# Softplus in a Mamba and mixture-of-experts kernel: two ScalarE operations in place of three

## The chip, the cores and the metric

The kernel runs on one core of a Trainium2 chip. The metric is the device time of one execution in microseconds (us). A core has TensorE (PE in the profile), VectorE (DVE), ScalarE (ACT), GpSimd (POOL) and SyncE (SP), which issues the DMAs; each works through its own list of instructions in the order in which the program gives them, and they wait for each other through semaphores.

## The reference

The input is x of 8 sequences (batches) of 1024 tokens and 256 channels, in float32. A layer has two parts: a two-way Mamba block and a mixture of experts, each between layernorms and with a residual. The change touches the Mamba block alone, and in it one line, the softplus:

```python
x = silu(causal_depthwise_conv(xz_half, conv_w, conv_b))
dbc = x @ Wx.T
delta, Bm, Cm = dbc[..., :64], dbc[..., 64:80], dbc[..., 80:]
delta = jax.nn.softplus(delta @ Wdt.T + b_dt)
dA = exp(delta[..., None] * A)                       # A = -exp(A_log)
bx = delta[..., None] * Bm[:, :, None, :] * x[..., None]
h = dA_t * h + bx_t                                  # for each token, 16 states
y = einsum("ben,bn->be", h, c) + Dp * x
```

## The kernel before

The 8 batches with two directions each make 16 passes w; w is 0 to 15. In a pass, 512 channels lie as 4 tiles c of 128 partitions, and the 1024 tokens as 2 halves s of 512 columns. For each pass and each of the 16 states n the engines run a loop over the 4 channel tiles. ScalarE makes `decay` (L1692), which is exp of delta times A, half by half. GpSimd makes `drive` (L1977, L1983), which is delta times x (the tile `xu`) times a row of B. VectorE runs the scan over the tokens from both (`h`, L1454, L1463 and L1466). TensorE transposes the states (`h_t`, L1238), and VectorE (L1475) or, for every third token block about, ScalarE and GpSimd together (`scaled` L1713, `y` L1995) add the transposed states, weighted with C, to `y`. There are 3 buffers of `decay`, 3 of `drive` and 3 of `h_t`, so each of these engines can run only a little ahead of the next.

Between these instructions stands all other work: the projections, the convolution, the experts, the norms, and the softplus. Its place is fixed by a table of numbers written out by hand (`AT`), one number for each piece and engine; a piece stands in an engine's list at that slot. One softplus is a piece for a pass, a channel tile and a half, so there are 16 x 4 x 2 = 128 of them. It has four steps on three engines. TensorE's `dt_mm` (L1294) writes a PSUM bank (`side`, of which there are 2 for all this work). ScalarE's `softplus` (L1791, L1793, L1795) reads it and leaves a part of the result in `log_parts`, which the profile shows as `prep_work`. VectorE's `delta` (L1513) reads both, writes delta and so frees the bank. GpSimd's `u_mul` (L2007) multiplies x by delta for the two halves of a tile in one instruction; from pass 1 on delta also goes to memory and back, to be loaded for `decay`. In pass 0 all this stands ahead of the first scans, at the start of the program; later passes are prepared while the scans of the pass before run.

ScalarE can hold several tables of functions, one at a time. The kernel loads the one with Exp and Ln after each use of another.

Of the kernel before, what the change touches and what calls it, by code (L numbers as in the profile page):

```python
# [9 lines left out]
ALU = mybir.AluOpType  # L10
ACT = mybir.ActivationFunctionType
# [540 lines left out]
        873, 1018, 1020, 1022, 1025, 1175, 1176, 1177, 1180, 1240, 1241, 1242, 1243],  # L552
    "tok_apply": [1154, 1155, 1167, 1169],
}

TAIL_USE = 1153

# [22 lines left out]
class Plan:  # L580
# [23 lines left out]
    def nth(self, piece, *index):  # L604
        return self.at[piece, index]
# [152 lines left out]
def mamba_moe(nc, x, w_in_t, chan, wx_t, wdt_t, w_out_t, router_w, router_b, w1, b1_t, w2, b2, out):  # L758
# [47 lines left out]
    nth = plan.nth  # L806


    bank_of, bank_before, filled = {}, {}, {}
# [26 lines left out]
    with ctx:  # L836
# [78 lines left out]
        log_parts = xz_pad[:, PAD:PAD + L]  # L915
# [19 lines left out]
        side = [ctx.enter_context(nc.psum_tensor(f"side{i}", [P, BANK], F32)) for i in range(N_SIDE)]  # L935
# [36 lines left out]
        soft_step = sem("soft_step")  # L972
# [450 lines left out]
        def dve_program(dve):  # L1423
# [77 lines left out]
            def side_piece(piece, index):  # L1501
                if piece == "delta":
                    w, c, s = index
                    half_of = slice(s * BANK, (s + 1) * BANK)
# [4 lines left out]
                    elif w % 2 and w > 1:  # L1509
                        dve.wait_ge(done["u_mul"], nth("u_mul", w - 1, EC - 1))  # L1510
                        dve.wait_ge(done["delta_store"], 16 * nth("delta_store", w - 1, EC - 1))
                    into = prep_half if w else delta[:, c, :]
                    op = dve.e.scalar_tensor_tensor(out=into[:, half_of], in0=side[bank_of["dt_mm", index]][:, :],  # L1513
                                                    scalar=0.0, in1=log_parts[:, half_of], op0=ALU.max, op1=ALU.add)
                elif piece in ("tok_stats", "ln_stats"):
                    kind, at, j = index
                    src, dst, first, n, (stats, mv, rstd, shift) = norm_io(kind, at)
# [8 lines left out]
                    for tb in (first + 2 * j, first + 2 * j + 1):  # L1526
                        op = dve.e.bn_stats(stats[:, tb, :], src[:, tb, :])
                elif piece in ("tok_var", "ln_var"):
# [4 lines left out]
                    for tb in range(first, first + n):  # L1533
                        op = dve.e.bn_aggr(mv[:, tb, :], stats[:, tb, :])
                elif piece == "tap":
                    w, c, s = index
# [3 lines left out]
                    for k in range(1, TAPS):  # L1540
                        at = PAD - (TAPS - 1 - k) + s * BANK
                        into = bank[:, :] if k + 1 < TAPS else xu[:, 0, c, s * BANK:(s + 1) * BANK]
                        op = dve.e.scalar_tensor_tensor(out=into, in0=xz_of(w, c)[:, at:at + BANK],
                                                        scalar=chan_col(0, c, CHAN_CONV_W + k), in1=bank[:, :],
                                                        op0=ALU.mult, op1=ALU.add)
# [3 lines left out]
                elif piece == "gate":  # L1549
                    b, s, c = index  # L1550
# [3 lines left out]
                    op = dve.e.tensor_tensor(its, side[bank_of["y_turn", index]][:, :], its, ALU.mult)  # L1554
                elif piece == "res_add":
                    b, s, j = index
# [6 lines left out]
                    else:  # L1563
                        dve.wait_ge(own_res_in[s], 16 * QB // 2)
                    op = dve.e.tensor_tensor(acc_of(b)[:, at:at + 2, :].rearrange("p b d -> p (b d)"), bank[:, :],
                                             tokens_of(b, at, 2), ALU.add)
                elif piece == "peak":
# [8 lines left out]
                    op = dve.e.tensor_tensor(logits[:, :, :], logits[:, :, :], wide(), ALU.subtract)  # L1576
                elif piece == "top1":
                    b, = index
                    dve.wait_ge(done["probs"], nth("probs", b))
                    if b:  # L1580
# [6 lines left out]
                    op = dve.e.scalar_tensor_tensor(out=mix[:, :, 0:E], in0=sel1[:, :, :], scalar=-2.0,  # L1587
                                                    in1=logits[:, :, :], op0=ALU.mult, op1=ALU.add)
                elif piece == "top2":
# [6 lines left out]
                    op = dve.e.tensor_tensor(mix[:, :, 0:E], logits[:, :, :], both[:, :, :], ALU.mult)  # L1596
                elif piece == "slots":
# [5 lines left out]
                    if b:  # L1603
                        for i in range(N_FOUND):
# [14 lines left out]
                                                       in1=ranks, op0=ALU.mult, op1=ALU.add))  # L1619
# [3 lines left out]
                    op = dve.e.tensor_copy(slot_i[:, :, :], slot_f[:, :, :])  # L1623
                elif piece == "owners":
# [11 lines left out]
                    for r, sel in enumerate((sel1, sel2)):  # L1636
                        ordered(dve.e.tensor_tensor(cand[:, :, :], logits[:, :, :], sel[:, :, :], ALU.mult))
                        op = dve.e.tensor_reduce(share[:, b % 2, r, :], cand[:, :, :], AX_X, ALU.add)
                        if r + 1 < TOP:
                            ordered(op)  # L1640
                elif piece == "comb":
# [5 lines left out]
                    op = dve.e.tensor_tensor(its, side[bank_of["comb_mm", index]][:, :], its, ALU.add)  # L1647
                elif piece == "fin_add":
                    b, s, j = index
# [4 lines left out]
                    op = dve.e.tensor_tensor(acc_of(b)[:, at:at + 2, :].rearrange("p b d -> p (b d)"), bank[:, :],  # L1654
                                             x1_of(b)[:, at:at + 2, :].rearrange("p b d -> p (b d)"), ALU.add)
# [16 lines left out]
        def act_program(act):  # L1672
# [42 lines left out]
            def side_piece(piece, index):  # L1715
                if piece == "xn_copy":
                    b, s, c = index
# [3 lines left out]
                    op = act.e.copy(xn_t[:, c, s * BANK:(s + 1) * BANK], side[bank_of["xn_turn", index]][:, :])  # L1721
                elif piece == "xz_copy":
                    b, c, s = index
# [6 lines left out]
                    op = act.e.copy(xz_of(2 * b, c)[:, PAD + s * BANK:PAD + (s + 1) * BANK], side[bank_of["proj", index]][:, :])  # L1730
                elif piece == "conv_copy":
                    w, c, s = index
                    d = w % 2
                    act.wait_ge(done["conv_mm"], nth("conv_mm", w, c, s, 1))
                    if w >= 2:
                        act.wait_ge(drive_made, (w - 1) * UNITS)
                    op = act.e.activation(xu[:, d, c, s * BANK:(s + 1) * BANK], side[bank_of["conv_mm", (w, c, s)]][:, :],
                                          ACT.Identity, bias=chan_col(d, c, CHAN_CONV_B))
                elif piece == "tap0":
                    w, c, s = index  # L1740
# [5 lines left out]
                    op = act.e.activation(bank[:, :], xz_of(w, c)[:, at:at + BANK], ACT.Identity,  # L1746
                                          scale=chan_col(0, c, CHAN_CONV_W), bias=chan_col(0, c, CHAN_CONV_B))
                elif piece == "neg_a":
# [5 lines left out]
                    op = act.e.mul(neg_a[:, :, :, :], neg_a[:, :, :, :], -1.0)  # L1754
                elif piece == "silu_x":
                    w, s = index
# [5 lines left out]
                    op = act.e.activation(its, its, ACT.Silu)  # L1762
                    if w or s == NH - 1:
                        act.e.preload_act_table_set("natural_log_exp_and_others")
                elif piece == "dbc_copy":
                    w, s = index
# [5 lines left out]
                    op = act.e.copy(dbc[0:NP, s * BANK:(s + 1) * BANK], side[bank_of["dbc_mm", index]][0:NP, :])  # L1772
                elif piece == "c_copy":
                    w, s = index
                    act.wait_ge(done["c_turn"], nth("c_turn", w, s))
                    if w >= 2:
                        act.wait_ge(summed, summed_to((w - 1) * TILES - 1))
                        act.wait_ge(tile_scaled, pooled_to((w - 1) * TILES - 1))
                    op = act.e.copy(c_col[:, w % 2, s * QB:(s + 1) * QB, :],
                                    side[bank_of["c_turn", index]][:, 0:QB * NP].rearrange(  # L1780
                                        "p (q k) -> p q k", q=QB)[:, :, DTR + N:NP])
                elif piece == "softplus":
                    w, c, s = index
                    log_part = log_parts[:, s * BANK:(s + 1) * BANK]
# [2 lines left out]
                        act.wait_ge(done["delta"], nth("delta", w, c - 1, s))  # L1787
                    elif w % 2 == 0:
                        act.wait_ge(done["xz_store"], 16 * nth("xz_store", w // 2, EC - 1))
                    done_before = 2 * (nth("softplus", w, c, s) - 1)  # L1790
                    act.e.activation(log_part, side[bank_of["dt_mm", index]][:, :], ACT.Abs).then_inc(soft_step, 1)  # L1791
                    act.wait_ge(soft_step, done_before + 1)
                    act.e.activation(log_part, log_part, ACT.Exp, scale=-1.0).then_inc(soft_step, 1)  # L1793
                    act.wait_ge(soft_step, done_before + 2)
                    op = act.e.activation(log_part, log_part, ACT.Ln, bias=1.0)  # L1795
                elif piece == "z_copy":
                    b, s, c = index
# [7 lines left out]
                    op = act.e.copy(z_of(b, s)[:, c, :], side[bank_of["z_mm", index]][:, :])  # L1805
                elif piece == "z_silu":
                    b, s = index
                    act.wait_ge(done["z_copy"], nth("z_copy", b, s, EC - 1))
                    op = act.e.activation(z_of(b, s), z_of(b, s), ACT.Silu)
                    act.e.preload_act_table_set("natural_log_exp_and_others")  # L1810
                elif piece == "out_copy":
# [9 lines left out]
                    op = act.e.mul(acc_of(b)[:, tile_of(b, i), :], side[bank_of["out_mm", index]][:, 0:D], 0.5)  # L1821
                elif piece == "xn2_copy":
                    b, s, c = index
# [7 lines left out]
                    op = act.e.copy(xn2_of(b)[:, c, t:t + BANK], side[bank_of["xn2_turn", index]][:, :])  # L1831
                elif piece in ("tok_apply", "ln_apply"):
# [6 lines left out]
                    if kind in ("post", "fin"):  # L1839
                        into = free_bank(act, piece, index)[:, :].rearrange("p (r d) -> p r d", d=D)  # L1840
                    elif kind == "pre":
                        into = tokens_of(at[0], first + 2 * j, 2).rearrange("p (r d) -> p r d", d=D)
                    else:
                        into = dst[:, 2 * j:2 * j + 2, :]
                    for r in range(2):
                        tb = first + 2 * j + r
                        op = act.e.activation(into[:, r, :], src[:, tb, :], ACT.Identity, scale=rstd[:, tb:tb + 1],
                                              bias=shift[:, tb:tb + 1])
                elif piece == "probs":
                    b, = index  # L1850
                    act.wait_ge(done["peak"], nth("peak", b))
                    op = act.e.activation(logits[:, :, :], logits[:, :, :], ACT.Exp)
                elif piece == "mix_copy":
# [6 lines left out]
                    op = act.e.copy(mix_t[:, q * BANK:(q + 1) * BANK], side[bank_of["mix_turn", index]][0:NX, :])  # L1860
                elif piece == "h1_bias":
# [5 lines left out]
                    else:  # L1867
                        act.wait_ge(done["y_turn"], nth("y_turn", b, 0 if b == LAST else NH - 1, EC - 1, 1))
                    op = act.e.activation(h1_of(b)[:, m, :], side[bank_of["h1_mm", index]][:, :], ACT.Identity,
                                          bias=b1_sb[:, m, NX - 1:NX])  # L1870
                elif piece == "gelu":
                    b, g = index
                    act.wait_ge(done["h1_bias"], nth("h1_bias", b, g, HC - 1))
                    op = act.e.activation(h1_of(b)[:, :, :], h1_of(b)[:, :, :], ACT.Gelu)
                    if (b, g) != (LAST, NH - 1):
                        act.e.preload_act_table_set("natural_log_exp_and_others")
                elif piece == "eo_copy":
# [4 lines left out]
                    op = act.e.copy(acc_of(b)[:, tb:tb + 2, :].rearrange("p b d -> p (b d)"),  # L1882
                                    side[bank_of["eo_mm", index]][:, :])
                elif piece == "share_diag":
# [7 lines left out]
                    for r in range(TOP):  # L1892
                        op = act.e.mul(diag[:, i % 2, r, :], ident[:, :], share[:, b % 2, r, tile_of(b, i):tile_of(b, i) + 1])
                elif piece == "bias_copy":
                    b, = index
                    act.wait_ge(done["bias_mm"], nth("bias_mm", b))
                    if b:
                        act.wait_ge(done["r1_copy"], nth("r1_copy", b - 1, BLOCKS - 1))
                    op = act.e.copy(b1_blocks[:, :, :].rearrange("p m j -> p (m j)"),
                                    side[bank_of["bias_mm", index]][:, 0:HC * SLOTS])  # L1900
                elif piece == "xs_copy":
                    b, G, c = index
# [28 lines left out]
                elif piece == "rgelu":  # L1931
# [4 lines left out]
                    op = act.e.activation(its, its, ACT.Gelu)  # L1936
# [501 lines left out]
```

## Time and profile before

| | |
|---|---|
| median of 3 runs | 4375.84 us (4371.07 to 4379.16) |
| the profiled execution's own time | 4368.3 us |
| its span in the profile | 4367.0 us |
| busy: PE, DVE, POOL, ACT | 82%, 85%, 83%, 72% |

The profile is of one execution. Its own time stands 1.3 us over its span and 7.5 us under the median. Busy shares are those of the whole span. The chain of work that ended last is followed back from the last instruction, at each step to what released it or to the instruction before it on its engine. In a timeline, the brackets give the idle time of the engine ahead of an instruction and what ended it.

### The profile page before, as it was taken

The page shows a single profiled execution, that of the slowest core. Times are in us where ns is not written, and L with a number is a line of the kernel's source. Part 1 is how long each engine was busy: PE and PEld are TensorE (multiplying, and loading weights), DVE is VectorE, ACT ScalarE, POOL GpSimd, SP SyncE. Part 2 cuts the span into 40 slices and gives each one's busy share as a digit, 9 for nine tenths or more (in the row PEclk, how much of TensorE's full clock was granted, in tenths as well). Part 3 has the DMA queues.
Part 4 walks back from the last instruction along what each step waited for, and adds up shares of the span by engine and source line. Part 5 has one row for each costly group of instructions (what it writes and reads, how often), then busy time and mean ns, then how long its engine had stood idle before and what let it go on. Part 6 is the DMA issues. An engine that isn't in the chain of part 4 may idle for free.

```text
span 4367.0 us, 58183 instructions
## 1 busy us (share of the span) xinstructions
PE 3587.1 (82%) x18192; PEld 2572.1 (59%) x18192; DVE 3692.7 (85%) x4568; ACT 3162.5 (72%) x5296; POOL 3645.2 (83%) x2205
## 2 busy tenths in 40 slices
PE   5677687988879897798879887798987989878887
PEld 2444455666546655576555774556755666557766
DVE  5899998998988979889898988988989897989720
ACT  5667576887768867688766887768876787768643
POOL 5899988998888988889888989888997898889721
PEclk8778797999979999899979998899998999889988
DMA  5232232566335654357433674445643566426555
GB/s 176 85 111 97 100 134 81 197 197 216 128 116 172 205 198 130 110 182 240 159 130 131 195 235 144 142 140 188 229 157 109 169 201 221 137 95 215 181 178 186
DMA packets 374654, 700.87 MB, mean 160 GB/s; under 512 B 31809, under 2 KB 205386, under 8 KB 370378
## 3 DMA queue, kind: packets, MB, share of 16 engines
q1 hardware_dynamic: 362058, 663.59, 46.1%
q0 software_dynamic: 12288, 33.57, 2.3%
q8 instruction: 145, 2.38, 0.2%
q14 instruction: 163, 1.34, 0.1%
HBM read 527.72 MB, written 169.35 MB: 160 GB/s over the span
## 4 chain that ended last, share of the span: by engine, by line
PE 27%; DVE 23%; POOL 20%; issue 14%; ACT 13%; DMA 3%; DVEq 0%; SPq 0%; POOLq 0%; ACTq 0%
POOL drive L1977 10%; DVE h L1466 8%; DVE h L1463 7%; PE h_t L1238 5%; PE side L1272 4%; DVE y L1475 4%; ACT decay L1692 3%; POOL y L1995 3%; PE side L1411 3%; POOL xs_dram L2053 2%; PE side L1403 2%; PE side L1327 1%; PE side L1300 1%; PE side L1279 1%; ACT scaled L1713 1%
## 5 line engine op out<-in xcount | busy, mean ns | idle before, releaser
L1977 POOL TENSOR_TENSOR drive<-xu,b_row 128x1024 f32<-128x1024 f32 x960 | 2263.0, 2362 | 284.9 <-DVE h L1466 185.1
L1692 ACT ACTIVATE decay<-delta,neg_a 128x512 f32<-128x512 f32 x2048 | 1397.1, 692 | 674.4 <-DVE h L1466 400.5
L1238 PE MATMUL h_t<-ident,h 128*128 128x128 f32 x8192 | 1281.9, 300 | 513.8 <-DVE y L1475 209.0
L1238 PEld LDWEIGHTS h_t<-ident,h 128*128 128x128 f32 x8192 | 1049.0, 155 | 897.9 <-DVE y L1475 303.0
L1475 DVE SCALAR_TENSOR_TENSOR y<-h_t,c_col,y 128x512 f32<-128x512 f32 x1368 | 996.0, 728 | 131.8 <-PE h_t L1238 127.6
L1995 POOL TENSOR_TENSOR y<-y,scaled 128x512 f32<-128x512 f32 x616 | 784.8, 1274 | 71.1 <-ACT scaled L1713 69.6
L1466 DVE TENSOR_TENSOR_SCAN h<-decay,h,drive 128x512 f32<-128x512 f32 x512 | 652.4, 1274 | 32.8 <-ACT decay L1692 20.9
L1466 DVE TENSOR_TENSOR_SCAN h<-decay,drive 128x512 f32<-128x512 f32 x512 | 618.2, 1207 | 51.0 <-POOL drive L1977 26.6
L1463 DVE TENSOR_TENSOR_SCAN h<-decay,h,drive 128x512 f32<-128x512 f32 x448 | 571.6, 1276 | 57.5 <-ACT decay L1692 47.2
L1463 DVE TENSOR_TENSOR_SCAN h<-decay,drive 128x512 f32<-128x512 f32 x448 | 541.3, 1208 | 67.0 <-POOL drive L1977 35.2
L1713 ACT ACTIVATE scaled<-h_t,c_col 128x512 f32<-128x512 f32 x616 | 415.6, 675 | 101.6 <-PE h_t L1238 101.5
L1272 PE MATMUL side<-prep_work,conv_diag 128*128 128x512 f32 x960 | 458.5, 611 | 10.8 <-DMA prep_work<-xz_dram 4.5
L1411 PE MATMUL side<-expert_w,work 128*128 128x256 f32 x1304 | 336.2, 409 | 30.1 <-ACT xn_t L1911 10.5
L1403 PE MATMUL side<-xn_t,expert_w 128*128 128x128 f32 x2608 | 335.7, 278 | 25.1 <-ACT work L1929 7.1
L1403 PEld LDWEIGHTS side<-xn_t,expert_w 128*128 128x128 f32 x2608 | 312.6, 193 | 40.6 <-ACT work L1929 12.0
L1411 PEld LDWEIGHTS side<-expert_w,work 128*128 128x128 f32 x1304 | 258.7, 207 | 77.3 <-ACT xn_t L1911 12.1
L1272 PEld LDWEIGHTS side<-prep_work,conv_diag 128*128 128x128 f32 x960 | 174.1, 196 | 167.4 <-issue 157.9
L2065 POOL DMA_INDIRECT work<-ys_dram,slot_i x128 | 123.0, 961 | 164.2 <-DMA ys_dram<-work 109.3
L1929 ACT ACTIVATE work<-side,b_blocks 128x128 f32<-128x128 f32 x644 | 183.3, 373 | 32.2 <-PE side L1403 31.3
L1294 PE MATMUL side<-dbc,wdt_sb 97*128 97x512 f32 x256 | 158.3, 715 | 24.0 <-ACT xn_t L1911 10.9
L1983 POOL TENSOR_TENSOR drive<-xu,b_row 128x1024 f32<-128x1024 f32 x64 | 151.0, 2365 | 12.2 <-DVE h L1454 11.3
L2053 POOL DMA_INDIRECT xs_dram<-work,slot_i x112 | 110.3, 984 | 58.4 <-issue 30.5
(297 smaller groups left out, 4366.7 us busy)
## 6 DMA issues: line engine op xcount, KB each, us to landing
expert_w<-in_w SPq DMA_DIRECT2D x350, 512.0 KB, 4.5
b_row<-b_dram SPq DMA_DIRECT2D x240, 512.0 KB, 4.1
x_dram<-xu SPq DMA_DIRECT2D x16, 2048.0 KB, 7.7
delta_dram<-prep_work SPq DMA_DIRECT2D x60, 512.0 KB, 4.2
delta<-delta_dram SPq DMA_DIRECT2D x60, 512.0 KB, 4.6
ys_dram<-work SPq DMA_DIRECT2D x40, 512.0 KB, 6.4
work<-xs_dram SPq DMA_DIRECT2D x38, 512.0 KB, 4.6
h<-in_w SPq DMA_DIRECT2D x34, 512.0 KB, 4.8
```

What stands on the lines that cost most here:

```text
L1238: t = pe.e.transpose(h_t[i % N_H_T][:, c * P:(c + 1) * P], its_h[:, c, :], ident[:, :])
L1272: mm = pe.e.matmul(bank[:, :], conv_diag[:, k, :], xz_pad[:, at:at + BANK], start=(k == 0), stop=(k == TAPS - 1))
L1403: mm = pe.e.matmul(bank[:, m * P:(m + 1) * P], wi[:, k, m * P:(m + 1) * P], xn2_t[:, k, at:at + P], start=(k == 0), stop=(k == DC - 1))
L1411: mm = pe.e.matmul(bank[:, q % 2 * D:(q % 2 + 1) * D], h1_blocks(b, G)[:, q, m, :], wo[:, m, :], start=(m == 0), stop=(m == HC - 1))
L1463: return dve.e.tensor_tensor_scan(o[:, ::-1], its_decay[:, ::-1], v[:, ::-1], before, ALU.mult, ALU.add)
L1466: return dve.e.tensor_tensor_scan(o, its_decay, v, before, ALU.mult, ALU.add)
L1475: dve.e.scalar_tensor_tensor(out=y[:, tb, :], in0=h_t[i % N_H_T][:, :], scalar=c_n, in1=y[:, tb, :], op0=ALU.mult, op1=ALU.add).then_inc(s ...
L1692: act.e.activation(decay[:, i % N_DECAY, :], delta[:, c, its], ACT.Exp, scale=neg_a[:, c, w % 2, n:n + 1]).then_inc(decay_made, 1)
L1713: act.e.mul(into, h_t[i % N_H_T][:, :], c_col[:, w % 2, tb, n:n + 1]).then_inc(tile_scaled, 1)
L1977: op = pool.e.tensor_tensor(drive[:, k % N_DRIVE, :], xu[:, w % 2, c, :], b_row[:, row % N_B_ROW, :], ALU.mult)
L1995: pool.e.tensor_tensor(y[:, tb, :], y[:, tb, :], scaled[:, at % N_SCALED, :], ALU.add).then_inc(gathered, 1)
L2053: pool.e.indirect_dma_start(out=xs_dram, out_offset=bass.IndirectOffsetOnAxis(ap=slot_i[:, r, tb:tb + 1], axis=0), in_=tokens_of(b, tb, 1) ...
```

## The change

Before, softplus(x) was max(x, 0) + ln(1 + exp(-|x|)): ScalarE made |x| out of PSUM, then Exp with the scale -1, then Ln with the bias 1, and VectorE put max(x, 0) to it. Now it is max(min(ln(1 + exp(x)), 17), x): ScalarE makes Exp out of PSUM and then Ln, and VectorE takes the smaller of that and 17, and then the larger of that and x. Over 17, where the result is x to within what float32 shows, x is the larger. In VectorE's instruction the PSUM bank was the first tensor operand and is now the second.

```diff
--- before.py
+++ after.py
@@ -553,6 +553,8 @@
     "tok_apply": [1154, 1155, 1167, 1169],
 }
 
+SOFT_MAX = 17.0
+
 TAIL_USE = 1153
 
 EMPTIED_BY = {"xn_turn": "xn_copy", "proj": "xz_copy", "dbc_mm": "dbc_copy", "c_turn": "c_copy", "dt_mm": "delta",
@@ -1510,8 +1512,8 @@
                         dve.wait_ge(done["u_mul"], nth("u_mul", w - 1, EC - 1))
                         dve.wait_ge(done["delta_store"], 16 * nth("delta_store", w - 1, EC - 1))
                     into = prep_half if w else delta[:, c, :]
-                    op = dve.e.scalar_tensor_tensor(out=into[:, half_of], in0=side[bank_of["dt_mm", index]][:, :],
-                                                    scalar=0.0, in1=log_parts[:, half_of], op0=ALU.max, op1=ALU.add)
+                    op = dve.e.scalar_tensor_tensor(out=into[:, half_of], in0=log_parts[:, half_of], scalar=SOFT_MAX,
+                                                    in1=side[bank_of["dt_mm", index]][:, :], op0=ALU.min, op1=ALU.max)
                 elif piece in ("tok_stats", "ln_stats"):
                     kind, at, j = index
                     src, dst, first, n, (stats, mv, rstd, shift) = norm_io(kind, at)
@@ -1787,11 +1789,8 @@
                         act.wait_ge(done["delta"], nth("delta", w, c - 1, s))
                     elif w % 2 == 0:
                         act.wait_ge(done["xz_store"], 16 * nth("xz_store", w // 2, EC - 1))
-                    done_before = 2 * (nth("softplus", w, c, s) - 1)
-                    act.e.activation(log_part, side[bank_of["dt_mm", index]][:, :], ACT.Abs).then_inc(soft_step, 1)
-                    act.wait_ge(soft_step, done_before + 1)
-                    act.e.activation(log_part, log_part, ACT.Exp, scale=-1.0).then_inc(soft_step, 1)
-                    act.wait_ge(soft_step, done_before + 2)
+                    act.e.activation(log_part, side[bank_of["dt_mm", index]][:, :], ACT.Exp).then_inc(soft_step, 1)
+                    act.wait_ge(soft_step, nth("softplus", w, c, s))
                     op = act.e.activation(log_part, log_part, ACT.Ln, bias=1.0)
                 elif piece == "z_copy":
                     b, s, c = index
```

ScalarE's rows below are the first two pieces `softplus` (pass 0, tile 0, both halves) and the first `decay` behind them, each with the semaphores that it waits for. Before:

```order
L1791 ACTIVATE prep_work<-side 128x512 [waits s_xz_store,s_dt_mm]
L1793 ACTIVATE prep_work<-prep_work 128x512 [waits soft_step]
L1795 ACTIVATE prep_work<-prep_work 128x512 [waits soft_step]
L1791 ACTIVATE prep_work<-side 128x512 [waits s_dt_mm]
L1793 ACTIVATE prep_work<-prep_work 128x512 [waits soft_step]
L1795 ACTIVATE prep_work<-prep_work 128x512 [waits soft_step]
L1692 ACTIVATE decay<-delta,neg_a 128x512 [waits s_delta,s_neg_a]
```

Now:

```order
L1792 ACTIVATE prep_work<-side 128x512 [waits s_xz_store,s_dt_mm]
L1794 ACTIVATE prep_work<-prep_work 128x512 [waits soft_step]
L1792 ACTIVATE prep_work<-side 128x512 [waits s_dt_mm]
L1794 ACTIVATE prep_work<-prep_work 128x512 [waits soft_step]
L1694 ACTIVATE decay<-delta,neg_a 128x512 [waits s_delta,s_neg_a]
```

One row of each piece has gone, and nothing else stands elsewhere: ScalarE's list is 128 instructions shorter, it has the same table loads, and TensorE, VectorE, GpSimd and SyncE have the same instructions in the same order, but for the operands of VectorE's `delta`. (Line numbers behind the first hunk are 2 higher, and those behind the second 1 lower.)

## Rows read from the trace of the kernel before

**Rows 1.** The page's head and its section 1: busy time of each engine, share, instructions
```profile
span 4367.0 us, 58183 instructions
...
PE 3587.1 (82%) x18192; PEld 2572.1 (59%) x18192; DVE 3692.7 (85%) x4568; ACT 3162.5 (72%) x5296; POOL 3645.2 (83%) x2205
```

**Rows 2.** The chain of work that ended last: share of the span by engine
```profile
PE 27%; DVE 23%; POOL 20%; issue 14%; ACT 13%; DMA 3%; DVEq 0%; SPq 0%; POOLq 0%; ACTq 0%
```

**Rows 3.** Waits: who waited for whom, total us, times, longest us
```profile
ACT decay L1692 <- DVE h L1466: 400.5, 432, 5.0
...
ACT decay L1692 <- DVE h L1463: 234.4, 298, 7.3
```

**Rows 4.** ACT's groups by form: count, busy us, mean ns, idle before
```profile
L1692 ACT ACTIVATE decay<-delta,neg_a 128x512 f32<-128x512 f32 x2048 | 1397.1, 692 | 674.4 <-DVE h L1466 400.5 <-DVE h L1463 234.4 <-DVE h L1454 27.5
...
L1793 ACT ACTIVATE prep_work<-prep_work 128x512 f32<-128x512 f32 x128 | 80.7, 631 | 4.1
L1795 ACT ACTIVATE prep_work<-prep_work 128x512 f32<-128x512 f32 x128 | 80.7, 631 | 4.0
L1791 ACT ACTIVATE prep_work<-side 128x512 f32<-128x512 f32 x128 | 75.5, 590 | 23.2 <-PE side L1294 22.8
```

**Rows 5.** Timeline of ACT at its second softplus: start us, us, what
```profile
54.70 0.63 ACT L1795 ACTIVATE prep_work<-prep_work 128x512 f32<-128x512 f32 x1
55.23 0.58 ACT L1791 ACTIVATE prep_work<-side 128x512 f32<-128x512 f32 x1
55.84 0.63 ACT L1793 ACTIVATE prep_work<-prep_work 128x512 f32<-128x512 f32 x1
56.51 0.63 ACT L1795 ACTIVATE prep_work<-prep_work 128x512 f32<-128x512 f32 x1
```

**Rows 6.** DVE's groups by form: count, busy us, mean ns, idle before
```profile
L1475 DVE SCALAR_TENSOR_TENSOR y<-h_t,c_col,y 128x512 f32<-128x512 f32 x1368 | 996.0, 728 | 131.8 <-PE h_t L1238 127.6 <-POOL y L1995 2.5
...
L1513 DVE SCALAR_TENSOR_TENSOR prep_work<-side,prep_work 128x512 f32<-128x512 f32 x120 | 81.3, 680 | 12.1 <-ACT prep_work L1795 11.9
...
L1543 DVE SCALAR_TENSOR_TENSOR xu<-h,chan_sb,side 128x512 f32<-128x512 f32 x8 | 6.0, 748 | 0.3
```

**Rows 7.** Timeline of POOL, start of the program: start us, us, what, idle before
```profile
57.94 2.35 POOL L2007 TENSOR_TENSOR xu<-xu,delta 128x1024 f32<-128x1024 f32 x1 [37.58 <-DVE delta L1513]
60.25 1.04 POOL L2034 TENSOR_TENSOR conv_diag<-ident,chan_sb 128x512 f32<-128x512 f32 x1
62.77 2.35 POOL L2007 TENSOR_TENSOR xu<-xu,delta 128x1024 f32<-128x1024 f32 x1 [1.49 <-DVE delta L1513]
...
70.70 4.66 POOL L2007 TENSOR_TENSOR xu<-xu,delta 128x1024 f32<-128x1024 f32 x2
75.31 9.25 POOL L1977 TENSOR_TENSOR drive<-xu,b_row 128x1024 f32<-128x1024 f32 x4
```

**Rows 8.** Timeline of DVE, the same stretch
```profile
72.00 0.67 DVE L1513 SCALAR_TENSOR_TENSOR delta<-side,prep_work 128x512 f32<-128x512 f32 x1
...
77.76 1.22 DVE L1466 TENSOR_TENSOR_SCAN h<-decay,drive 128x512 f32<-128x512 f32 x1 [3.91 <-POOL drive L1977]
```

**Rows 9.** The chain that ended last: its first and last piece of L1793
```profile
54.04 0.64 ACT prep_work L1793
...
3736.77 0.64 ACT prep_work L1793
```

**Rows 10.** Timeline, instructions that end ACT's part of the chain, with idle before them
```profile
1451.88 1.28 DVE L1463 TENSOR_TENSOR_SCAN h<-decay,h,drive 128x512 f32<-128x512 f32 x1 [2.34 <-ACT decay L1692]
...
2512.42 0.69 DVE L1513 SCALAR_TENSOR_TENSOR prep_work<-side,prep_work 128x512 f32<-128x512 f32 x1 [2.39 <-ACT prep_work L1795]
...
3550.66 1.28 POOL L1995 TENSOR_TENSOR y<-y,scaled 128x512 f32<-128x512 f32 x1 [2.59 <-ACT scaled L1713]
```

**Rows 11.** Timeline of DVE: two places where it has next to no idle time
```profile
2159.06 0.69 DVE L1513 SCALAR_TENSOR_TENSOR prep_work<-side,prep_work 128x512 f32<-128x512 f32 x1
...
3202.65 1.21 DVE L1466 TENSOR_TENSOR_SCAN h<-decay,drive 128x512 f32<-128x512 f32 x1
```

## The prediction

> **What bounds the kernel now.** The page's head comes first: no engine is the bound of the whole span. VectorE is busy for 85% of it, GpSimd for 83%, TensorE for 82% and ScalarE for 72% [rows 1]. The chain of work that ended last says how this is to be read: it passes from engine to engine, and 13% of the span in it is ScalarE's [rows 2]. Next come the waits. ScalarE, ahead of a `decay`, waits 400.5 + 234.4 us for a scan, 432 + 298 times [rows 3]. That is 730 of its 2048 `decay` instructions [rows 4]: at about one in three (0.36) ScalarE is early, and what it does faster there only lengthens its wait. At the others it works through a queue, and something may wait for it. So the 128 shorter softplus pieces are not worth their busy time. They are worth what lies on the chain, and of that only as much as the engine that waits for ScalarE had idle.
>
> **What the change removes.** One softplus piece is three instructions on ScalarE: L1791 out of PSUM, mean 590 ns, then L1793 and L1795 out of SBUF, 631 ns each [rows 4]. Each waits for the one before. In the timeline L1793 starts at 55.84 us and L1795 at 56.51, so a dependent step takes 0.67 us from start to start; L1791, which depends on nothing just before it, starts at 55.23, 0.10 before L1795 of the piece before ends (54.70 + 0.63) [rows 5]. What stays is one instruction out of PSUM and one out of SBUF. If Exp out of PSUM takes what L1791 takes, the loss of a step is 0.66 us a piece (631 ns and some 30 ns until the next starts), 128 x 0.66 = 84.5 us of ScalarE's time in all. The trace has no Exp out of PSUM. Its bounds are L1791's 590 ns below, and above the 692 ns of `decay`, an Exp out of SBUF with a scale for each partition [rows 4]; by the upper one a piece saves 0.66 - 0.10 = 0.56 us. I take 590: shape, source and immediate scale are those of L1791.
>
> The Trainium skill, ScalarE: Activation LUTs, "Same chain, other wiring", has every function at one element per cycle and lane. By this rule Exp out of PSUM costs what the absolute value costs, and a piece saves 0.66 us. The trace agrees as far as it goes: L1793 (Exp) and L1795 (Ln) both show 631 ns [rows 4]. The same page, "What ACT_TABLE_LOAD costs", gives 186 ns + 0.833 ns per element for an ACTIVATE with immediate scale and bias, an estimate of 612 ns at 512 columns, whatever the source. By that a piece would save 0.64 us; the measured 590 and 631 decide.
>
> **What the change adds.** No instruction and no table load: the order has as many loads as before. VectorE's `delta` has min and max for max and add, and its PSUM operand is the second instead of the first. Before it takes 680 ns. The nearest rows with a PSUM tensor first and second are L1475 with 728 ns and L1543 with 748, both with a scalar for each partition [rows 6]. Their difference is 20 ns; a price under nothing I exclude, since 680 ns is already the least of the three. I take 20 ns, with 0 as the other bound. All 128 of them make 2.6 us. I count a quarter as on the path, since VectorE holds 23% of the chain [rows 2]: 0.7 us against the change.
>
> **The start of the program.** Here ScalarE sets the pace, since the first scans wait for softplus. GpSimd's first `u_mul` starts at 57.94 us, behind two pieces. It then makes a `conv_diag`, sits idle for 1.49 us and starts the second `u_mul` at 62.77, behind four pieces [rows 7]. With four steps fewer that one's delta comes 4 x 0.66 = 2.64 us earlier. GpSimd's own queue allows 2 x 0.66 + 1.49 = 2.81 us, which is more, so the delta decides: 2.6 us. After that GpSimd has no idle time until 75.31 + 9.25 = 84.56 [rows 7], and VectorE waits for its `drive` (3.91 us before 77.76) [rows 8], so the gain is kept. One thing could take from it. The fourth `u_mul` starts at 70.70 + 2.33 = 73.03 and would start at 70.4. Its delta, the eighth, stands on VectorE between scans at 72.00 [rows 8]. It moves with the scans to 69.4 and ends at 70.0, 0.4 us in time.
>
> **The passes behind it.** In the chain L1793 is met 23 times of 128, first at 54.04 and last at 3736.77 us [rows 9]. Two of the 23 are in the start. For each of the other 21 I went forward along the chain to the first instruction of another engine, and read that engine's idle time before it. This is what its own queue lets it gain. At 15 it is enough for all the pieces ahead: 2.34, 2.39 and 2.59 us in the rows shown [rows 10], where one or two pieces save 0.66 or 1.32. That is 15 x 0.66 = 9.9 us. At the other 6 there is little: five have about 0.1 us or none, as at 2159.06, where VectorE has just ended an instruction, and at 3202.65 [rows 11], and one 0.39; together 0.6 us. So the queues of the next engines leave 10.5 of 21 x 0.66 = 13.9 us. Two things take from that. ScalarE, when earlier, meets a wait for a scan buffer between softplus and the end of its stretch: at most the share of 0.36 from above. And a path that ran beside the chain, and that I cannot follow, may end later than the shortened one. I take a quarter off for both, a choice between none and 0.36: 7.9 us.
>
> **The sum.** 2.6 + 7.9 - 0.7 = 9.8 us. The profiled execution's own time is 4368.3 us, so its counterpart would be 4358.5. It stands 7.5 us under the median of the runs shown, and the same gain on that median gives 4375.84 - 9.8 = 4366.0 us, 0.22% less. About 0.2%, 8.7 us, is what a measurement of this kernel can tell from no change, so the forecast lies almost on the edge.
>
> **Rivals.**
> *The slack swallows it.* ScalarE, 72% busy and early at a third of its `decay`s, is not what most stages wait for; VectorE and GpSimd, at 85% and 83%, go on as before. Then the start remains with 2.6 us, and the 20 ns of `delta` cost between 0.7 and 2.6: a gain of 0 to 2, with a little from the passes up to 6 us; 4370 to 4376. For it speaks that only 23 of 128 are on the chain, and that six of those meet a full queue. Against it: 15 places with over 0.66 us idle behind them.
> *All of it counts.* All 23 steps come out of the time, 15.2 us, and the start gives 1.3 more than its two steps in the chain (2.64 against 1.32): 16.5 us, 4359.3. For it: the places are those at which ScalarE was late. Against: the six full queues.
> *Slower.* VectorE's `delta` with the PSUM bank as second operand takes much longer than 680 ns. It frees the bank for TensorE, and GpSimd waits for it. With a quarter of 128 on the path, 32 of them, against a gain of 10.5 us otherwise, the change is without effect at 10.5 / 32 = 0.33 us more for each, and slower by 0.2% at 0.60 us more. If it went in two passes, and took 1.36 us, the time would be 4375.84 - 10.5 + 32 x 0.68 = 4387. The rows with PSUM second (748 ns) speak against it [rows 6].
> *The step is not saved.* Exp out of PSUM would have to take 590 + 660 ns for that; nothing in the rows, with 692 ns at most for such an instruction, speaks for it, and it has no chance of its own.
>
> **How the numbers follow.** A gain near the sum, 6 to 14 us: 0.54. Swallowed: 0.27. All of it: 0.13. Slower: 0.06. The likeliest gives 4366.0. Of its 0.54, rather more than two thirds, 0.37, lie beyond 8.7 us. With 0.13 that is 0.50 for faster; 0.44 is left for no difference, and 0.06 for slower. The range goes from a gain of 17.5, which is all of it and 1 us for the spread of medians, to the upper end of the swallowed case: 4358 to 4376. What it leaves out is the slower case and the edges of the others.
>
> **What the profile afterwards would show.** ScalarE with 5168 instructions and 80 us less busy time; the Exp out of PSUM near 590 ns, at most 692; `delta` between 680 and 700 ns; the second `u_mul` on GpSimd at about 60.1 us, and everything to 84 us earlier by 2.6. ScalarE's waits for scans should grow by most of the 84 us, since only a tenth of it is gained. VectorE's wait for L1795's successor, 11.9 us in pass 1 on [rows 6], should shrink by half or more. The prediction is wrong if the start gives less than 2 us, which would mean that another wait stands right behind; or if the rest of the gain is under 3 us or over 14, which would mean that the idle time of the next engine is no measure of what is gained.

## The result

The changed kernel takes 4364.86 us in the median of 20 runs (4357.38 to 4373.52), the kernel before 4375.07 us in 20 runs (4371.07 to 4383.15). The ratio is 0.9974 with a 95% interval of 0.9967 to 0.9981: 11.4 us less, 8.3 to 14.4. A second comparison, 12 runs against 19, gave 0.998 (0.9969 to 0.999), 8.7 us less, 4.4 to 13.6. All gains here are (1 - ratio) times the median of before; the ratio is formed from all the runs and not from the two medians, so the difference of the medians is up to 4 us off it (10.2 us in the first comparison). Two executions that took over twice the usual time, one of the kernel before (9046.76 us) and one of a kernel below (11018.61 us), are left out of all medians. The forecast was 9.8 us, 4366.0 on the median shown.

The profiled execution's span is 4363.0 us. These are the page's head, its section 1 and the chain's shares by engine, for the changed kernel; they answer to [rows 1, 2].

```profile
span 4363.0 us, 58055 instructions
...
PE 3581.1 (82%) x18192; PEld 2572.4 (59%) x18192; DVE 3692.2 (85%) x4568; ACT 3088.2 (71%) x5168; POOL 3644.6 (84%) x2205
...
PE 27%; DVE 22%; POOL 21%; issue 14%; ACT 12%; DMA 3%; DVEq 0%; SPq 0%; another core or an unknown queue 0%; POOLq 0%; ACTq 0%
```

ScalarE has 128 instructions and 74.3 us of busy time less. The other engines have as many instructions as before. Of 74 us, 11 reach the time.

The groups of ScalarE and `delta` on VectorE from pass 1 on, by form, answer to [rows 4, 6]. The last row is from the view of one line: least, median and longest duration in ns, then the first and the last start in us.

```profile
L1694 ACT ACTIVATE decay<-delta,neg_a 128x512 f32<-128x512 f32 x2048 | 1399.0, 692 | 705.5 <-DVE h L1468 420.2 <-DVE h L1465 245.4 <-DVE h L1456 22.1
...
L1794 ACT ACTIVATE prep_work<-prep_work 128x512 f32<-128x512 f32 x128 | 80.7, 631 | 4.1
L1792 ACT ACTIVATE prep_work<-side 128x512 f32<-128x512 f32 x128 | 75.7, 592 | 34.0 <-PE side L1296 33.7
...
L1515 DVE SCALAR_TENSOR_TENSOR prep_work<-prep_work,side x120: 657/677/689, 203.5 to 3753.3; 128x512 f32<-128x512 f32 x120
```

Exp out of PSUM (L1792) takes 592 ns, and `delta` with PSUM as second operand 677, not 700. Before, the same view of `delta` read:

```profile
L1513 DVE SCALAR_TENSOR_TENSOR prep_work<-side,prep_work x120: 656/680/694, 206.9 to 3764.0; 128x512 f32<-128x512 f32 x120
```

So the first `delta` of pass 1 stands 206.9 - 203.5 = 3.4 us earlier and the last of pass 15 10.7 us earlier (3764.0 - 3753.3), while the spans differ by 4.0 us alone. The rest of the lead goes between 3764 us and the last expert sums, where there is no softplus. The chain's last DMA of an expert store shows what is left of it by then. First before, then after:

```profile
4325.32 2.51 DMA ys_dram<-work
```

```profile
4321.30 2.51 DMA ys_dram<-work
```

The lead here is 4.0 us. I do not put this loss to the change. In the second profiled execution of the changed kernel the last `delta` of pass 15 starts at 3750.9 us, 13.1 us earlier than before, and the span is 4355.4 us, still 11.6 shorter. The profiled execution of before took 4368.3 us, 6.8 under the median of its kernel, and that of after lies at its median; single executions of one kernel differ by as much as the whole effect (12 us from lowest to highest before, 16 after). The times of many runs decide, the traces tell where.

The start on GpSimd and on ScalarE, timelines of the changed kernel [rows 5, 7]:

```profile
56.63 2.35 POOL L2006 TENSOR_TENSOR xu<-xu,delta 128x1024 f32<-128x1024 f32 x1 [35.99 <-DVE delta L1515]
...
60.59 2.35 POOL L2006 TENSOR_TENSOR xu<-xu,delta 128x1024 f32<-128x1024 f32 x1 [0.60 <-DVE delta L1515]
...
68.52 4.64 POOL L2006 TENSOR_TENSOR xu<-xu,delta 128x1024 f32<-128x1024 f32 x2
```

```profile
54.06 0.63 ACT L1794 ACTIVATE prep_work<-prep_work 128x512 f32<-128x512 f32 x1
54.59 0.58 ACT L1792 ACTIVATE prep_work<-side 128x512 f32<-128x512 f32 x1
...
56.63 0.60 ACT L1792 ACTIVATE prep_work<-side 128x512 f32<-128x512 f32 x1 [0.21 <-PE side L1296]
```

The first `u_mul` is 57.94 - 56.63 = 1.31 us earlier, as two steps make it. The second is 62.77 - 60.59 = 2.18 us earlier and not 2.64. The third piece shows why. ScalarE, faster now, waits 0.21 us for the matmul that fills its PSUM bank, where before it had no idle time:

```profile
57.66 0.58 ACT L1791 ACTIVATE prep_work<-side 128x512 f32<-128x512 f32 x1
```

So the third piece starts 57.66 - 56.63 = 1.03 us earlier and not 1.32. TensorE in its turn had waited 1.21 us for a `delta` to free one of the two banks. The fourth piece starts 60.07 - 58.53 = 1.54 us earlier, where three removed steps would be 1.98. The lead of 2.18 holds to the fourth `u_mul` (70.70 - 68.52).

Behind the start, the three instructions of [rows 10] in the changed kernel, each from its engine's timeline:

```profile
1443.97 1.28 DVE L1465 TENSOR_TENSOR_SCAN h<-decay,h,drive 128x512 f32<-128x512 f32 x1 [1.50 <-ACT decay L1694]
...
2503.22 0.69 DVE L1515 SCALAR_TENSOR_TENSOR prep_work<-prep_work,side 128x512 f32<-128x512 f32 x1 [1.74 <-ACT prep_work L1794]
...
3542.28 1.27 POOL L1994 TENSOR_TENSOR y<-y,scaled 128x512 f32<-128x512 f32 x1 [1.51 <-ACT scaled L1715]
```

Their idle time fell from 2.34 to 1.50, from 2.39 to 1.74 and from 2.59 to 1.51 us. The second has one piece ahead and gets its 0.65; the others have two, and get 0.84 and 1.08 of 1.32.

In the changed kernel's chain, L1794 is met 11 times; first and last:

```profile
54.06 0.63 ACT prep_work L1794
...
3540.39 0.03 ACT prep_work L1794
```

Before there were 23 [rows 9]. At 12 places net the chain has left ScalarE's softplus for another engine. Ten of the 11 are among the 23. A second execution of the changed kernel has 8, all among these 11.

### The profile page after: what moved, and what is told of

The parts are those of the page before. It is cut to its first block, busy times and chain, and to the rows that moved or that the text cites. A ratio compares the mean times of both kernels' runs of the same rounds, so it can differ in the third digit from the quotient of the medians.

```text
span 4363.0 us, 58055 instructions
## 1 busy us (share of the span) xinstructions
PE 3581.1 (82%) x18192; PEld 2572.4 (59%) x18192; DVE 3692.2 (85%) x4568; ACT 3088.2 (71%) x5168; POOL 3644.6 (84%) x2205
## 4 chain that ended last, share of the span: by engine, by line
PE 27%; DVE 22%; POOL 21%; issue 14%; ACT 12%; DMA 3%; DVEq 0%; SPq 0%; another core or an unknown queue 0%; POOLq 0%; ACTq 0%
POOL drive L1976 12%; DVE h L1468 8%; DVE h L1465 6%; PE h_t L1240 5%; PE side L1274 4%; DVE y L1477 4%; POOL y L1994 4%; PE side L1413 3%; ACT decay L1694 3%; PE side L1405 3%; POOL xs_dram L2052 2%; DMA expert_w<-in_w 1%; PE side L1329 1%; POOL xu L2006 1%; POOL work L2064 1%
## 5 line engine op out<-in xcount | busy, mean ns | idle before, releaser
L1694 ACT ACTIVATE decay<-delta,neg_a 128x512 f32<-128x512 f32 x2048 | 1399.0, 692 | 705.5 <-DVE h L1468 420.2
L1274 PE MATMUL side<-prep_work,conv_diag 128*128 128x512 f32 x960 | 458.4, 610 | 10.9 <-DMA prep_work<-xz_dram 4.1
L1413 PE MATMUL side<-expert_w,work 128*128 128x256 f32 x1304 | 334.4, 407 | 30.5 <-ACT xn_t L1910 10.5
```

The source lines that it names most:

```text
L1274: mm = pe.e.matmul(bank[:, :], conv_diag[:, k, :], xz_pad[:, at:at + BANK], start=(k == 0), stop=(k == TAPS - 1))
L1413: mm = pe.e.matmul(bank[:, q % 2 * D:(q % 2 + 1) * D], h1_blocks(b, G)[:, q, m, :], wo[:, m, :], start=(m == 0), stop=(m == HC - 1))
L1694: act.e.activation(decay[:, i % N_DECAY, :], delta[:, c, its], ACT.Exp, scale=neg_a[:, c, w % 2, n:n + 1]).then_inc(decay_made, 1)
```

## Experiments: which pieces carry it

The theory of the prediction is that a piece is worth its step where the chain passes through it, and nothing elsewhere. Its rival: the chain is that of one execution, one among many of near-equal length, and every piece carries a like small share. Three kernels split the change by pieces. `short(w, c, s)` says which pieces have two steps; k is the number of the piece in the order of the program, and each kernel has one of the three return lines. `steps_to` counts the steps of all pieces before this one. `delta` has the formula that belongs to its piece. The edit, against the kernel before and shortened:

```diff
+ON_CHAIN = (33, 34, 35, 40, 41, 48, 50, 51, 67, 73, 75, 82, 88, 90, 99, 106, 107, 116, 117, 121, 123)
+
+def short(w, c, s):
+    k = 8 * w + 2 * c + s
+    return k in ON_CHAIN                  # chain21
+    return w > 0 and k not in ON_CHAIN    # others99
+    return w == 0                         # start8
...
-                    done_before = 2 * (nth("softplus", w, c, s) - 1)
+                    done_before = steps_to(w, c, s)
+                    if short(w, c, s):
+                        act.e.activation(log_part, side[bank_of["dt_mm", index]][:, :], ACT.Exp).then_inc(soft_step, 1)
+                        act.wait_ge(soft_step, done_before + 1)
+                    else:
                         act.e.activation(log_part, side[bank_of["dt_mm", index]][:, :], ACT.Abs).then_inc(soft_step, 1)
...
```

**The 21 pieces on the chain behind the start.** Expected:

> Only the 21 softplus pieces behind the start whose Exp lies on the chain of the kernel before have two steps; the other 107 have three. Theory of the chain: what the change gains behind the start comes from these places, so this kernel gains 7 to 9 us of 4375. Rival, that every piece carries an equal small share since the chain of one execution is one of many near-equal ones: 21 of 120 of some 9 us, which is 1.6 us and not to be told from none.

Measured: 4369.21 us against 4376.35, ratio 0.9981 (0.9969 to 0.9992), 8.3 us less, 3.5 to 13.6. Half of the changed kernel's gain and more comes from 21 of 128 pieces. The rival's 1.6 us lies outside the interval.

**The 99 others.** Expected:

> The other 99 pieces behind the start have two steps; the start and the 21 pieces on the chain have three. Theory of the chain: 0 to 2 us of gain, not to be told from none. Rival of equal shares: 99 of 120 of some 9 us, which is 7.4 us.

Measured: 4374.05 us, ratio 0.9999 (0.9988 to 1.0009): 0.4 us less, between 5.3 less and 3.9 more (the medians are 2.3 us apart). The rival's 7.4 us lies outside. Nearly five times as many pieces give nothing that can be told, though ScalarE's busy time fell to 3105.4 us with them. The chain of this kernel still meets 18 of the 21 pieces, so it is much the same chain in another execution. The page of this kernel, section 1:

```profile
PE 3592.7 (82%) x18192; PEld 2580.6 (59%) x18192; DVE 3694.0 (84%) x4568; ACT 3105.4 (71%) x5197; POOL 3644.9 (83%) x2205
```

**The start.** Expected:

> Only the 8 pieces of pass 0 have two steps. The second u_mul of GpSimd starts 2.2 us earlier as in the changed kernel, and if nothing later takes it back the whole gains 2.2 us (0.05%). Rival, that a later wait takes the start's gain back: 0 us. By the time alone the two may not be told apart; the trace tells how far the lead holds.

Measured: 4375.12 us, ratio 0.9997 (0.9987 to 1.0007), 1.3 us less, between 5.7 less and 3.1 more. As expected, the time alone does not tell 2.2 from 0. GpSimd's timeline of this kernel shows the second `u_mul` at 60.29:

```profile
56.48 2.35 POOL L2029 TENSOR_TENSOR xu<-xu,delta 128x1024 f32<-128x1024 f32 x1 [35.64 <-DVE delta L1528]
...
60.29 2.35 POOL L2029 TENSOR_TENSOR xu<-xu,delta 128x1024 f32<-128x1024 f32 x1 [0.45 <-DVE delta L1528]
```

That is 2.48 us earlier than before, of which 0.15 stand ahead of the change (the first `u_mul` is 1.46 us earlier, two steps make 1.31). Some of the lead is still there behind 200 us: the first `delta` of pass 1 starts at 202.1 to 203.5 us in the four profiled executions whose start has two steps (this one, the changed kernel's two, and the last kernel below), and at 204.1 to 206.9 us in the five whose start is that of before, 2.9 us apart on average. The reverse does not hold: with a fourth step in all pieces (below) the last `delta` of pass 0 starts at 75.4 us, 3.4 later than before, and the first of pass 1 at 206.7, no later than before. Whether the lead lasts to the end is not shown: this execution's time, 4373.6 us, says nothing of 2 us.

The three add to 8.3 + 0.4 + 1.3 = 10.0 us, the whole to 11.4 and 8.7.

## Experiments: a step more

A slack that hides a shorter piece could be long or short. A fourth step tells, an Abs of exp(-|x|), which leaves the result as it is. The edit against the kernel before (that `done_before` now counts three steps a piece is left out):

```diff
                     act.e.activation(log_part, log_part, ACT.Exp, scale=-1.0).then_inc(soft_step, 1)
                     act.wait_ge(soft_step, done_before + 2)
+                    act.e.activation(log_part, log_part, ACT.Abs).then_inc(soft_step, 1)
+                    act.wait_ge(soft_step, done_before + 3)
                     op = act.e.activation(log_part, log_part, ACT.Ln, bias=1.0)
```

**In all pieces.** Expected:

> The kernel before with a fourth dependent step on ScalarE in every piece, 0.66 us each, 84 us in all; the result is the same. Theory of the chain: at least the 23 places on it cost 0.66 us each, 15 us, and some more join as they become late: 15 to 30 us slower. Rival, that ScalarE's busy time counts as a whole: 84 us slower. Rival, that slack swallows it: 0 to 5 us.

Measured: 4426.66 us in 4 runs, ratio 1.0116 (1.0097 to 1.0135), 50.8 us more. This was outside what I gave (15 to 30) and is between the theory and the rival. The trace of this kernel fits the mechanism; the number of places that join was misjudged. Its chain passes through 82 of the 128 pieces, and 82 x 0.66 = 54 us.

**In the 21 alone, and in the 99 alone.** The same edit under `if long(w, c, s)`, with the same two sets. Expected:

> A fourth dependent step of 0.66 us in the 21 pieces on the chain behind the start alone. Theory of the chain: each costs its full 0.66 us, 13.9 us slower. Rival of equal shares (the 50.6 us of all 128 pieces with four steps spread evenly): 21 of 128, 8.3 us.

Measured: 4391.9 us against 4377.7, ratio 1.0033 (1.0023 to 1.0043), 14.4 us more. 21 x 0.66 is 13.9. The rival's 8.3 lies outside the interval (10.1 to 18.8). This fits each piece on the chain paying its step in full; the interval allows 0.48 to 0.90 us for each.

> A fourth step in the 99 pieces that are not on the chain of the kernel before. Theory that these have a slack shorter than a step, so that they cost nothing when shortened but something when made longer: 50.6 for all, less 13.9 for the 21 and less 3 to 5 for the start, which is 30 to 34 us slower. Rival, that they have more slack than a step and the cost with four steps comes from the 21 and the start alone: 0 to 5 us.

Measured: 4413.64 us, ratio 1.0091 (1.0075 to 1.0106), 39.8 us more, 33 to 46, in 6 runs (the medians are 35.9 us apart). The forecast's 30 to 34 is at the lower end, the rival's 0 to 5 is out. So the pieces that gave nothing when they lost a step cost some 0.4 us each on average (39.8 / 99) when they got one. The chain of this kernel meets 50 of the 99: about half of them, at the least, had a slack shorter than the step. Together the two sets cost 54.2 us, the whole 50.8.

## Experiments: a step less still, and VectorE's part

**One step.** The changed kernel with Exp alone. It leaves out Ln, so its result is not the reference's:

```diff
-                    act.e.activation(log_part, side[bank_of["dt_mm", index]][:, :], ACT.Exp).then_inc(soft_step, 1)
-                    act.wait_ge(soft_step, nth("softplus", w, c, s))
-                    op = act.e.activation(log_part, log_part, ACT.Ln, bias=1.0)
+                    op = act.e.activation(log_part, side[bank_of["dt_mm", index]][:, :], ACT.Exp)
```

> The changed kernel without Ln, which leaves out a part of the computation: ScalarE makes Exp alone. Again 84 us less on ScalarE. Theory of the chain: 11 pieces of the changed kernel lie on its chain, so a further step gives at most 11 x 0.66 = 7.3 us, and 3 to 6 us likely; against the kernel before 14 to 17 us. Rival, that each step gives the same: another 11.4 us, 23 us against the kernel before.

Measured: 4358.03 us in 5 runs against 4377.7, ratio 0.9948 (0.9933 to 0.9962), 22.8 us less, 16.6 to 29.3. The theory's 14 is out, its 17 is at the edge, the rival's 23 fits. I ran it again with the changed kernel beside it:

> The changed kernel itself, beside the kernel with one step on the same chip: 11 us faster than before again, 8 to 14.

> The kernel with Exp alone again, which leaves out Ln, since its interval left both theories open. Theory of the chain: at most 7.3 us less than the changed kernel, 14 to 18 us under the kernel before. Rival, that each step removed gives the same: 11 us less than the changed kernel, 20 to 25 us under the kernel before.

Measured: the changed kernel 4363.71 us against 4372.34, ratio 0.998 (0.9969 to 0.999), 8.7 us less, at the lower end of what I expected; one step 4354.15, ratio 0.996 (0.9946 to 0.9973), 17.5 us less, 11.8 to 23.6. The medians of the two are 9.6 us apart, where the chain of the changed kernel allows 11 x 0.66 = 7.3 and I expected 3 to 6. In the first comparison they are 10.5 us apart, if the kernel with PSUM first (below, 4368.5 us) stands for the changed one. Both lie over my 3 to 6 and over the 7.3, the latter by less than the noise: with intervals of some 6 us on either side of each ratio, neither the theory nor the rival is excluded. The traces lean to the theory in one respect: of the pieces with one step, the chain passes through 6, and through 3 in the second execution. But the times stand nearer to the rival, and this stays open. What can be read is the start, where both theories agree. GpSimd's timeline with one step:

```profile
56.00 2.36 POOL L2004 TENSOR_TENSOR xu<-xu,delta 128x1024 f32<-128x1024 f32 x1 [35.64 <-DVE delta L1515]
...
59.30 2.37 POOL L2004 TENSOR_TENSOR xu<-xu,delta 128x1024 f32<-128x1024 f32 x1
```

The second `u_mul` comes 60.59 - 59.30 = 1.29 us earlier again and now has no idle time ahead of it: GpSimd's own queue sets it.

**VectorE's operands.** The changed kernel with PSUM as the first operand, and without the bound of 17:

```diff
-                    op = dve.e.scalar_tensor_tensor(out=into[:, half_of], in0=log_parts[:, half_of], scalar=SOFT_MAX,
-                                                    in1=side[bank_of["dt_mm", index]][:, :], op0=ALU.min, op1=ALU.max)
+                    op = dve.e.scalar_tensor_tensor(out=into[:, half_of], in0=side[bank_of["dt_mm", index]][:, :], scalar=0.0,
+                                                    in1=log_parts[:, half_of], op0=ALU.max, op1=ALU.max)
```

> The changed kernel with VectorE's delta as max(max(x, 0), ln(1 + exp(x))), with the PSUM bank as first operand as before, so without the bound of 17. The profile of the changed kernel shows 677 ns for delta with PSUM second, against 680 before. So the operands' order costs nothing: the same gain as the changed kernel's 11 us, and 675 to 690 ns. Rival, by the forecast's term: 20 ns each, 0.7 us, which only the rows can tell.

Measured: 4368.5 us against 4377.7, ratio 0.9977 (0.9968 to 0.9986), 10.1 us less, 6.1 to 14.0: the changed kernel's gain. The view of the line:

```profile
L1515 DVE SCALAR_TENSOR_TENSOR prep_work<-side,prep_work x120: 654/680/693, 202.1 to 3758.3; 128x512 f32<-128x512 f32 x120
```

The median is 680 ns with PSUM first, 677 with PSUM second. With an immediate scalar, the order of the operands costs nothing.

## Why the prediction was right, point by point

- **ScalarE's share.** The removed step was taken as 0.66 us from start to start. The first `u_mul` moved by 1.31 for two of them, and Exp out of PSUM took 592 ns where 590 was assumed. Right. (Exp out of SBUF took 631 ns before, so the source makes 39 ns and no one figure fits both.)
- **The start.** 2.64 us forecast, 2.18 measured in the trace of the start; in the time it can't be told from 0 (start8). The mechanism was right; what was left out is that ScalarE, once faster, waits for its matmul: 0.29 us of the lead are lost at the third piece and 0.15 at the fourth.
- **The passes.** 7.9 us forecast; 8.3 with the 21 pieces alone, 0.4 with the 99 others. This term carried the result, and the split shows it. The reading by the idle time of the next engine held in full at one of the three places shown (0.65) and in part at the other two (0.84 and 1.08 of 1.32, where the idle time was enough for all of it). That the quarter off was of the right size is shown only within the interval of chain21, 3.5 to 13.6 us.
- **VectorE.** 20 ns each and 0.7 us in all were forecast as a cost; the trace shows 3 ns less. The term was nought. Without it the sum would have been 10.5.
- **ScalarE's waits.** I said that waits for scans would grow by most of 84 us. They grew by 30.7 (400.5 + 234.4 to 420.2 + 245.4), those for the softplus matmul by 10.9 (22.8 to 33.7) [rows 4]. ScalarE's busy time fell by 74 and not by the forecast's 80: the removed instructions took 80.7 us, but the others took 2 us more in sum, and instructions overlap by 4 us less. Its idle time grew by 70 us in all (span less busy time, 1204.5 to 1274.8), and what is not named here is spread over its other groups. This side remark was wrong and carried nothing. VectorE's wait for the last step of softplus, from pass 1 on, fell from 11.9 to 5.7 us, by half as forecast.
- **The rivals.** That slack swallows it all (0 to 6 us) is excluded by the interval of the whole (8.3 to 14.4 us less); that of the second comparison, 4.4 to 13.6, leaves its upper end. That all 16.5 us count is excluded by both. The slower case rested on `delta`, which did not get longer.
- **The sum.** The mechanism was right, but that 9.8 stands so near to 11.4 is in part luck: the start came out 0.5 us lower than forecast, `delta`'s 0.7 was not there, the term of the passes rests on the chosen quarter and one generous reading, and the intervals are 6 and 9 us wide.

One reading in the term of the passes was too generous. At 15 places the next engine's idle time was said to be enough for all the pieces ahead. Two of the 15 (k = 40 and 41) stand ahead of one matmul, where TensorE had 0.84 us and not 1.32:

```profile
1112.74 2.07 PE L1294 MATMUL side<-dbc,wdt_sb 97*128 97x512 f32 x2 [0.84 <-ACT c_col L1779]
```

By the prediction's own rule that takes 0.48 us from the 10.5, and a quarter off the rest makes the term 7.5 and not 7.9.

The chain counted from both sides frames the gain here: 11 pieces on it after and 23 before, times 0.66, is 7.3 to 15.2 us, and 11.4 was measured. For a step more it is 15.2 to 54, and 50.8 was measured. I had not made this count beforehand, since it needs both traces. It is no strict bound. The second execution of the changed kernel has 8 pieces, 5.3 us. With a fourth step in the 99, the count allows 50 x 0.66 = 33 us, and 39.8 was measured. And the chain can miss a piece. Ahead of the second `u_mul` the chain of before shows

```profile
61.29 1.45 issue
```

where GpSimd's timeline has 1.49 us of waiting for `delta` [rows 7]. So the chain meets two pieces in the start, where the second `u_mul` waits for four.

No kernel here is shown to beat the changed one with the reference's result. The version with PSUM first, which lacks the bound of 17, ties with it.

## What to carry to other kernels

Where no engine is the bound, an instruction is worth its time at the places where the chain of work passes through it, up to the idle time of the next engine there; count these places instead of multiplying by all. The count is an estimate: a stretch of "issue" in the chain can hide a wait for the piece, and the engine's own timeline shows it. The same count does not hold for an addition: pieces with a slack shorter than the step join the chain, and here a step more cost over four times what a step less gave. When the effect is 0.25%, split the change by places and take many runs; one execution's trace shows where a lead arises, but not what is left of it at the end.

## What was not expected of the hardware

- VectorE's scalar_tensor_tensor on 128x512 float32 takes 677 ns with the PSUM tensor second and 680 with it first. Whether the 20 ns between the two nearest rows of before (748 and 728), both with a scalar for each partition, come from the order there was not tested.
- Executions of the kernel before, on one core with a fixed order, differ by 12 to 25 us in 4375 within groups of 19 to 29 runs, as much as the effect or twice; the widest group ran from 4366.75 to 4391.98 in 29 runs on one chip.
